# A four-layer recurrence and attention stack: the second layer's channel mix moved from the attention stream to the recurrence stream

## The reference

```python
# layers 0 and 2: time mix (a linear recurrence per head), then channel mix
xa = ln(x, ln1_w, ln1_b); sx = shift(xa) - xa          # shift: one token back
w, k, v, r, g = five low-rank mixed projections of xa, sx
for each token: out = r . (u * k v^T + s);  s = k v^T + w * s    # 32 heads of 8
x = x + (groupnorm(out) * silu(g)) @ Wo.T
xc = ln(x, ln2_w, ln2_b); sxc = shift(xc) - xc         # the channel mix
rr = sigmoid((xc + sxc * fr) @ fWr.T)
kk = square(relu((xc + sxc * fk) @ fWk.T))
x = x + rr * (kk @ fWv.T)
# layer 1: x = x + tanh(gate) * attention(x, ln(ctx), mask) @ Wo.T      (16 heads of 16)
# layer 3: x = x + attention(ln(x), ctx, mask) @ Wo + b;  x = x + mlp(ln(x))   (gelu, 1024)
```

## Time and profile before

| | us |
|---|---|
| median of 3 timed runs | 1272.8 (1272.34 to 1273.24) |
| profiled execution | 1274.41 |
| its span, first to last instruction | 1272.4 |
| TensorE busy | 1124.9 (88%) |
| VectorE busy | 859.5 (68%) |
| ScalarE busy | 501.7 (39%) |
| GpSimd busy | 106.6 (8%) |
| mean granted TensorE clock | 0.936 of full speed |

### The profile page before, as it was taken

How to read it: one execution, slowest core, us unless ns; L and a number is a source line. 1 busy time by engine, 2 the same in 40 slices (tenths; PEclk the granted TensorE clock), 3 DMA queues, 4 the chain that set the end, 5 groups by cost and what they waited for, 6 DMA issues and landing times.

```text
span 1272.4 us, 14341 instructions
## 1 busy us (share of the span) xinstructions
PE 1124.9 (88%) x5396; PEld 760.6 (60%) x5396; DVE 859.5 (68%) x1152; ACT 501.7 (39%) x1542; POOL 106.6 (8%) x92
## 2 busy tenths in 40 slices
PE   7867889997988999989898879899899998898888
PEld 4634656565755666657565565557656566477665
DVE  4599799688965798799745794466954569444320
ACT  1003125722582257325831624325533255232641
POOL 1020011001100100011000110001020010100000
PEclk8878889998999989989998999998999899899889
DMA  9100000000000000000000000000000000000000
GB/s 368 35 1 0 1 26 5 1 1 25 5 1 1 25 5 2 1 18 13 1 17 9 5 1 1 34 3 10 1 1 33 1 13 1 1 17 1 13 1 17
DMA packets 13895, 22.65 MB, mean 18 GB/s; under 512 B 3841, under 2 KB 10625, under 8 KB 13186
## 3 DMA queue, kind: packets, MB, share of 16 engines
q1 hardware_dynamic: 13826, 21.74, 5.1%
HBM read 16.48 MB, written 2.10 MB: 15 GB/s over the span
## 4 chain that ended last, share of the span: by engine, by line
PE 63%; DVE 24%; ACT 5%; issue 4%; POOL 3%; DMA 1%; SPq 0%; DVEq 0%; POOLq 0%; ACTq 0%
PE PA L1097 7%; PE QA L1003 6%; DVE S_ L509 5%; PE PB L1128 5%; PE QA L1315 5%; PE QB L990 4%; PE QB L1227 3%; PE PA L1036 3%; ACT big L923 3%; DVE az L378 3%; PE QA L1243 3%; DVE A L517 2%; PE QA L990 2%; DVE A L437 2%; PE QA L1306 2%
## 5 line engine op out<-in xcount | busy, mean ns | idle before, releaser
L923 ACT ACTIVATE big<-QB,nmax 128x128 f32<-128x128 f32 x512 | 181.4, 378 | 88.2 <-DVE nmax L632 88.1
L509 DVE TENSOR_TENSOR_SCAN S_<-W_,A 128x1024 f32<-128x1024 f32 x64 | 149.0, 2349 | 0.2
L1128 PE MATMUL PB<-A,common_w 128*128 128x256 f32 x512 | 131.3, 400 | 11.4 <-DVE A L517 11.4
L632 DVE TENSOR_REDUCE nmax<-QB 128x4 f32<-128x512 f32 x128 | 87.1, 685 | 65.6 <-PE QB L1227 41.4
L1128 PEld LDWEIGHTS PB<-A,common_w 128*128 128x128 f32 x512 | 98.3, 201 | 34.6 <-DVE A L517 15.1
L1097 PE MATMUL PA<-rwkv_w,X 128*128 128x256 f32 x384 | 100.8, 416 | 16.8 <-DVE X L416 16.6
L923 ACT ACTIVATION_READ_ACCUMULATOR big<-QB,nmax 128x1 f32 x512 | 111.8, 218 | 0.0
L1227 PE MATMUL QB<-big,QX 128*128 128x256 f32 x384 | 102.8, 392 | 0.0
L1097 PEld LDWEIGHTS PA<-rwkv_w,X 128*128 128x128 f32 x384 | 78.1, 209 | 34.3 <-DVE X L416 21.6
L1243 PE MATMUL QA<-common_w,big 128*128 128x128 f32 x512 | 83.8, 289 | 12.5 <-ACT XT L932 5.9
L1243 PEld LDWEIGHTS QA<-common_w,big 128*128 128x128 f32 x512 | 63.1, 147 | 40.5 <-issue 24.3
(11 more groups left out here) (160 smaller groups left out, 1871.5 us busy)
## 6 DMA issues: line engine op xcount, KB each, us to landing
rwkv_w<-in_rwkv_w SPq DMA_DIRECT2D x2, 2674.0 KB, 14.4
QX<-big SPq DMA_DIRECT2D x96, 32.0 KB, 1.9
attn_w<-in_attn_w SPq DMA_DIRECT2D x2, 1031.5 KB, 16.7
mlp_w<-in_mlp_w SPq DMA_DIRECT2D x1, 2052.0 KB, 23.5
X<-in_x SPq DMA_DIRECT2D x4, 512.0 KB, 13.1
ctx<-in_ctx SPq DMA_DIRECT2D x4, 512.0 KB, 4.2
ctx<-in_ctx_t SPq DMA_DIRECT2D x4, 512.0 KB, 3.5
out<-XT SPq DMA_DIRECT2D x8, 256.0 KB, 2.0
```

Of the source, the lines that this page charges most:

```text
L509: last = v.tensor_tensor_scan(S_[:, d].rearrange("p k t -> p (k t)"), W_[:].rearrange("p k t -> p (k t)"), A_[c % 2][:, d].rearrange("p k ...
L632: v.tensor_reduce(nmax[:, n % 2], bank(2 + n % 2).rearrange("p (j s) -> p j s", j=JH), AX.X, ALU.max, negate=True).then_inc(sem["a_max"], 1)
L923: last = s.activation(PR[:, n % 2, j], bank(2 + n % 2)[:, j * T:(j + 1) * T], ACT.Exp, bias=nmax[:, n % 2, j:j + 1], accum_out=den[:, b, h ...
L1128: last = t.matmul(y, ident, A_[c % 2][:, :, k], start=(c % 2 == 0 and k == 0), stop=False, skip_group_check=True)
```

## The change

The channel mix becomes a function on each engine, `channel_mix(u, n, w)`, with a name prefix for its semaphores and a dictionary `w` of buffers. Layer 0's attention units call it where the code stood before, with the same buffers. Layer 1's mixers (now of kind "mixer_ffn") call it at the end of `recurrence`, with buffers of the recurrence: A_0 and A_1, now one tile A2, hold CN, the two mixes and z; S_ holds the shift, kk and rr; and all three projections go to PB. Since they share PB, each half of fWr waits for ScalarE's relu of that half of fWk, and each half of fWv for the tanh of that half of fWr (`room`). The link between relu and square is a semaphore per half. All the dummy matmuls in the last unit's channel mix are gone. The wait for the stored output moves from VectorE's first mix to ScalarE's `norm_x`. All four `ORDER` strings are new, in the first layer too.

```diff
-for _kind in ("attn", "attn_mlp"): COUNTS[_kind].update(f_stats=1, ..., x_done=2)
+COUNTS["attn"].update(f_stats=1, ..., f_kr=2)
+COUNTS["mixer_ffn"] = dict(COUNTS["mixer"], g_stats=1, ..., g_kr=2)
-X_BEFORE = {("mixer", 0): 0, ("attn", 0): 1, ("mixer", 1): 3, ("attn_mlp", 1): 4}
+X_BEFORE = {("mixer", 0): 0, ("attn", 0): 1, ("mixer_ffn", 1): 3, ("attn_mlp", 1): 5}
+in_attn.update(k_out=QB, r_out=QA, v_out=QB)
+in_mixer.update(k_out=PB, r_out=PB, v_out=PB)
 # TensorE
+def channel_mix(u, n, w, free):
+    yield
+    pe.wait_ge(sem[n + "_z"], u.at(n + "_z", 1))
+    turn_tokens(lambda h: w["r_out"][:, h * 512:(h + 1) * 512], w["z"], sem[n + "_zT"])
+    yield
+    chan_proj(w["k_out"], rh_(u.layer, "fWk"), ..., sem[n + "_k"], wait for _mixed)
+    yield
+    yield from token_proj(w["r_out"], rh_(u.layer, "fWr"), ..., sem[n + "_r"], wait for _mixed,
+                          room=lambda k: None if free else pe.wait_ge(sem[n + "_kr"], u.at(n + "_kr", k + 1)))
+    yield
+    yield from token_proj(w["v_out"], rh_(u.layer, "fWv"), ..., sem[n + "_v"], wait for _kk,
+                          room=lambda k: None if free else pe.wait_ge(sem[n + "_rr"], u.at(n + "_rr", k + 1)))
 def recurrence(u):
     ...
+    if u.kind == "mixer_ffn":
+        yield from channel_mix(u, "g", in_mixer, False)
 def attn(u):
     if mlp:
         yield from keys_values(ctx_chan)
+    if not mlp:
+        yield from channel_mix(u, "f", in_attn, True)
     yield
-    pe.wait_ge(sem["f_z"], u.at("f_z", 1))
-    turn_tokens(bank, az, sem["f_zT"])
-    fill(16)
-    ...                      # fWk, fill(2), fWr, fWv, fill(24)
-    yield
     if mlp:
+        if u.index == len(ATTENTIONS) - 1:
+            pe.wait_ge(sem["r_gate"], MIXERS[-1].at("r_gate", 1))
+        pe.wait_ge(sem["a_v"], u.at("a_v", 1))
         pe.wait_ge(sem["a_z"], u.at("a_z", 1))
         turn_tokens(bank, az, sem["a_xT"])
```

More of the change, by code:

```diff
@@ L93 @@
 for _layer, _group in STEPS:
-    MIXERS.append(Unit("mixer", _layer, _group, MIXERS))
+    MIXERS.append(Unit("mixer_ffn" if _layer else "mixer", _layer, _group, MIXERS))
     ATTENTIONS.append(Unit("attn_mlp" if _layer else "attn", _layer, _group, ATTENTIONS))
@@ L115 @@
[L115 to L123 removed]
+        "RHHHHHHRRHRHRRRHHHAAAAAAAAAAAAAAAARAAAAAARAAAAAHAAAAAAAAAAHRAAARAAHAARRAHHHAAAAAAAAAAAAAAARAAAARAAAA"
@@ L207, in build @@
         RU = sb("RU", [T])
-        A_ = [sb(f"A_{i}", [DC, RS, T]) for i in range(2)]
+        A2 = sb("A2", [2, DC, RS, T])
+        A_ = [A2[:, i] for i in range(2)]
         S_ = sb("S_", [DC, RS, T])
@@ L440, in outer, with channel_mix @@
                                            ALU.mult)
+                def channel_mix(u, n, w, before):
+                    X, CN, CS, C5 = X2[u.lane], w["CN"], w["CS"], w["C5"]
+                    xf = X[:].rearrange("p b c -> p (b c)")
+                    yield
+                    x_ready(u, before)
+                    norm_stats(X, w["bn"], w["mv"], sem[n + "_stats"])
+                    yield
+                    dve.wait_ge(sem[n + "_rstd"], u.at(n + "_rstd", 1))
+                    v.tensor_copy(CN[:, :, :, 0], st_sb[u.lane][:, 0])
+                    norm_apply(w["z"], X, w["mv"], w["rstd"], sem[n + "_z"])
+                    yield
+                    shift(u, CS, CN, n + "_xn")
+                    mix(C5[0], CN, CS, r_(u.layer, "fk"), sem[n + "_mixed"])
+                    yield
+                    mix(C5[1], CN, CS, r_(u.layer, "fr"), sem[n + "_mixed"])
+                    for k in range(2):
+                        yield
+                        part = slice(512 * k, 512 * k + 512)
+                        dve.wait_ge(sem[n + "_rr"], u.at(n + "_rr", k + 1))
+                        dve.wait_ge(sem[n + "_v"], u.at(n + "_v", k + 1))
+                        link(v.scalar_tensor_tensor(w["cf"][:, part], w["CR"][:, part], 1.0, w["v_out"][:, part], ALU.add, ALU.mult))
+                        last = v.scalar_tensor_tensor(xf[:, part], w["cf"][:, part], 0.5, xf[:, part], ALU.mult, ALU.add)
+                    last.then_inc(lane_sem["x_done"][u.lane], 1)
                 def head(u):
@@ L560, in recurrence @@
                     last.then_inc(lane_sem["x_done"][u.lane], 1)
+                    if u.kind == "mixer_ffn":
+                        yield from channel_mix(u, "g", in_mixer, 1)
                 def attn(u):
@@ L579, in attn @@
                             dve.wait_ge(sem["bias_setup"], steps)
[L581 to L605 removed]
+                    if not mlp:
+                        yield from channel_mix(u, "f", in_attn, 0)
                     yield
@@ L668, in attn @@
                     yield
-                    x_ready(u, 1)
+                    x_ready(u, 0 if mlp else 1)
                     for k in range(2):
@@ L833, in recurrence @@
                             .then_inc(sem["r_yn"], 1)
+                    if u.kind == "mixer_ffn":
+                        yield from channel_mix(u, "g", in_mixer)
                 def attn(u):
@@ L844, in norm_x @@
                     def norm_x(k):
+                        if k == 0 and u.stored:
+                            act.wait_ge(sem["st_out"], 32 * u.stored)
                         for h in range(HALF):
@@ L885, in attn @@
                         yield from keys_values()
[L887 to L902 removed]
+                    if not mlp:
+                        yield from channel_mix(u, "f", in_attn)
                     yield
```

164 lines of the change are left out of this document (83 added, 81 removed).

## The result

The changed kernel takes 1228.8 us (median of 4 runs, 1226.8 to 1232.2) against 1272.6 for the kernel before (4 runs beside it): ratio 0.966, 95% interval 0.9635 to 0.968. The prediction, 1247 with a range of 1230 to 1272, had the direction and most of the mechanism, and was 18 us too high, just outside its range. The profiled execution took 1226.78 us, 47.6 less than that of before. In this document one execution that ran at a far lower clock throughout (experiment 12, 1628 us at a mean of 0.63) is left out.

The account below looks back on a forecast made before the run. TensorE was taken to set the second layer's pace, through idle time, low clock and the end. Terms -11.3 - 20.7 - 5.4 + 12 = -25.4 took 1274.4 to 1249.0, so 1247 us for the timed median, 1.6 lower; range 1230 to 1272.

Parts of the forecast that it names:

- What bounds the kernel: Second layer: TensorE sets the pace; its idle time, low clock and the end can be gained, a shorter VectorE chain gains nothing.
- Term 1: The end, from unit 6's last MLP matmul to attention 7's transposes: 39.15 us becomes 20.4; net -11.3 us, including 1.7 lost.
- Term 2: Waits before the MLP's transposes (L1296) in units 4, 5 and 6: covered by moved work, with their low clock; -20.7 us.
- Term 4: New waits for ScalarE's evacuation of shared PB and at the last Wo pair behind VectorE's late normalise(1): 0 to 27, taken +12 us.
- Term 3: Two waits at the channel mix of units 5 and 6 with their low clock: between 0 and -10.9 us, taken -5.4.
- Term 5: The first layer's changed order and mix 4 woven into attention 3: 0, with 6 us either way.
- rival C: Slower: the recurrence's stream becomes the bound, the next unit's first outer product waiting for the mix; about 1291 us, chance 0.12.
- The fills: The 42 dummy matmuls of the last unit's mix lie in waits already counted, so removing them changes nothing.
- Rival A: The wait only changes place, to the last Wo pair: 1258 to 1268, say 1261 us, chance 0.20.
- Rival D: Without fills the last unit runs at the lower clock in more of its attention: +6.8, 1254 us, chance 0.05.
- Rival B: No change: the end's overlap is paid back by low clock and new waits; 1272 us, chance 0.07.

Follow-up runs that it names:

- experiment 12: Linked GpSimd operations added to each second-layer mix's deviation: four in the kernel before 1292.0 us; in the changed kernel four 1248.2 us, two 0.9676, one 1228.2 us.
- experiment 5: The changed kernel's code in the order of before, but with the new order for the last recurrence, last MLP and last mix; 1276.2 us.
- experiment 6: The changed kernel with the order of before for the last recurrence's fourth round, the last MLP and the last mix, without fills; 1257.5 us.
- experiment 4: The changed kernel with the MLP's transposes of attentions 4, 5 and 6 put back ahead of the last chunk's products and both halves of Wg; 1253.3 us.
- experiment 7: The changed kernel with the MLP's second product put wholly ahead of the mix's transposes on TensorE in units 5, 6 and 7; 1238.1 us.
- experiment 1: The changed kernel's code, without the mix's fills, with every step at its place in the kernel before; 1287.5 us.
- experiment 8: The kernel before, mix in the attention stream with its 42 fills, given the new strings as far as that stream's order allows; 1264.5 us.
- experiment 9: The kernel before with the new strings as far as the attention stream allows, and without the last mix's 42 fills; 1271.0 us.
- experiment 2: The changed kernel with the old strings up to the end of attention 2 and the new ones after; 1228.5 us.
- experiment 10: The changed kernel with the 42 fills put back in the last unit's mix; 1236.4 us.

## Why the prediction was wrong

*What bounds the kernel* was right: TensorE's idle time and its clock in the second layer. VectorE's busy time didn't move (859.5 to 863.1), and TensorE's span did.

*Term 1, -11.3: right.* The stretch was put at 20.4 us and measured 20.6. That the part put in alone gave just 11.3 us (experiment 5) is luck: it holds 4.5 us of new waits, has the low clock behind the gap, and is measured against a tail without fills. Taken out of the change the same part costs 28.7 (experiment 6). The 1.7 us for a low clock behind the gap was not due in the change: the gap was 2.23 us long and the clock stayed at full speed there.

*Term 2, -20.7: right.* All three waits are gone, by the mechanism named; taken out alone it costs 24.5 us, with 16.3 us of waits where 14.0 were assumed (experiment 4). The price of a wait with its low clock was right for these waits, 1.5 to 1; elsewhere it was higher, 1.8 (experiment 12) and 2.3 (experiment 7, 9.3 us for 4.0).

*Term 4, +12: this step failed in size.* It was a cost for waits between nothing and 27 us, and I chose near the middle from caution although its nearest row, 0.56 us, spoke for the low end. Measured: at most 0.3 us a unit at the second Wo pair (758.10 above), none at fWr or fWv for ScalarE. This one term is 12 of the 18 us by which the forecast was too high. VectorE's late `normalise(1)` stands behind work that TensorE has meanwhile.

*Term 3, -5.4: this step failed in size and in reach.* Both waits went whole, 10.9. With term 4 at nothing, term 3 whole and no 1.7, the same sum is -13.0 - 20.7 - 10.9 = -44.6, and measured were -47.6. That this comes out so near is luck in part: it does not make the parts independent, and the sum leaves out unit 4's other waits. I had listed one wait of that unit, and the trace of before has three more:

```profile
674.46 3.78 PE L1097 MATMUL PA<-rwkv_w,X 128*128 128x256 f32 x8 [3.76 <-DVE X L416]
...
701.24 0.39 PE L1221 MATMUL QB<-mrow,first_row 128*128 128x512 bf16 x1 [2.32 <-ACT big L923]
...
730.60 0.39 PE L1221 MATMUL QB<-mrow,first_row 128*128 128x512 bf16 x1 [3.41 <-ACT big L923]
```

In the change no wait of that unit is over 1.2 us, and its stretch fell by 22.9 us (168.8 to 145.9), where the terms hold 7.3 for it (5.59 and 1.7 of clock). In experiment 1, the old order, all three are back.

What I had not seen either is what lets the waits go. I treated those of term 3 as two gaps at the mix of units 5 and 6, and the stream as a matter of buffers. In fact the attention stream's order forbids the mix of unit u to start before the MLP of unit u-1 has ended, for TensorE and VectorE alike, and it holds keys and values in front of it. In the recurrence's stream all of these can stand between the mix's links. Experiments 8 and 9 price it, with the change's strings: 36 us if the old stream keeps its fills, 42 if it doesn't, of 44 in all.

*Term 5, 0: half right.* The first layer is worth nothing (experiment 2). But "mix 4 is woven into attention 3", which I left without a sign here and held for the danger in rival C, lies in the stretch that holds the largest single piece, 14.6 us (experiment 8).

*The fills: right for the changed kernel, for an incomplete reason.* They did lie in waits before; they also held the clock there (experiment 9). The change makes them useless by filling the same gaps with products, where their work would cost 7.6 us.

*Rival A* (the wait changes place) did not come in the change, though it is what happened in experiment 5, where half of the change was made. *Rival C* (slower) fell: VectorE's first outer product of a unit never waited for the mix. *Rival D* (the fills mattered) fell with experiment 10. *Rival B* (no change) fell by 44 us; the code alone, in the old order, is even slower (experiment 1).

The section that the prediction cites from the Trainium skill, "HAM oscillation — how this bites in real kernels" in "TensorE: Matmul & The Clock Gate", has waits of about 3 to 5 us in its own example. The traces agree for gaps of such a size and above: behind the 3.73 us of the earlier trace rows it was 0.76, and the transposes behind each of the three waits of 5.4 us in experiment 4 took 1.97 us instead of 1.04. That gaps of 2.05 and 2.71 us brought it too is shown by the earlier trace rows and not by that section, and one of 2.23 us brought it in one kernel and not in another: see the last section.

What stays open: the 42 us are shown as one piece and by unit, not divided among TensorE's, VectorE's and ScalarE's share of the freedom; on TensorE alone, with the MLP's second product only, it is 9.3 (experiment 7). No run separates what shared PB costs. And no run shows how good an order the attention stream allows at best: the 9 us are those of one order, made from the change's strings.

## What to carry to other kernels

When an in-order stream holds a chain of short dependent steps (here a layer norm, a mix, three products), ask first what its neighbours in that stream forbid it to stand beside. Moving it to a stream whose neighbours are independent gained nothing by itself (1287.5 us in the old places, without the fills), and the new places, as far as the old stream allows them, gave 9 us; together they gave 44. So price a change of stream with its order as one thing. Where the engine is full everywhere else, a wait cost 1.5, 1.8 and 2.3 times its length here (experiments 4, 12 and 7), so count it at more than its length, and don't add parts: taken out one at a time, three parts of this change cost 24.5, 28.7 and 36 us of a gain of 44. And fills are worth what surrounds them: keep them while a step waits alone, drop them when real work fills its gaps.

## What the runs showed of the hardware

The same gap brings the lower clock or doesn't. In the change and in experiment 5 the work in front of the last attention's transposes is the same for 20 us, and the idle time is 2.23 us in both. Four us from these transposes on, in the change and then in experiment 5:

```profile
1124.60:1128.60 4.00, 3.94 (x20) 2.76 (x21) 0.36 (x1) 2.73 (x3) 0.00 (x0) 1.00 0.00 0
```

```profile
1173.60:1177.60 4.00, 3.92 (x16) 3.48 (x17) 0.00 (x0) 2.79 (x3) 0.00 (x0) 0.57 0.00 0
```

Clock 1.00 in the one, 0.57 in the other; 1.07 us for the eight transposes and 1.85. Before the change a 2.05 us gap had brought 0.62. So these runs give no way to forecast the low clock for a single gap of this size; behind the three waits of 5.4 us it came each time (experiment 4). In the change it fell 9 us later, to 0.50 from 1134 us on, behind waits of 0.85 and 0.95 us.

VectorE's scans grew from 2349 to 2472 ns on average. Where GpSimd's product of the values (L764) falls beside them, two took 6.53 us in place of 4.47. GpSimd and then VectorE in the change:

```profile
1051.06 2.36 POOL L764 TENSOR_TENSOR V_<-V_,RU 128x1024 f32<-128x1024 f32 x1 [35.73 <-DVE A L453]
```

```profile
1051.22 6.53 DVE L549 TENSOR_TENSOR_SCAN S_<-W_,A 128x1024 f32<-128x1024 f32 x2
```

The slow scans are those beside that product: seven of the change's 64 took 4.0 to 4.4 us, where those beside no GpSimd work took 2.27 on average; before there were two of 4.0 and two of 2.9. With 64 scans that is 8 us of VectorE time, which cost nothing measurable here, since VectorE has 36 to 46 us to spare in each full unit.
